# A two-layer gated cross-attention and expert kernel: when GpSimd runs beside VectorE, how the slot one-hots are made, and what the first loads and the first tile share the queues with

## The reference

```python
x = x + tanh(g_xattn[0]) * L0_xattn(layernorm(x), ctx)      # both sides quantised to fp8 by blocks, then x @ ctx^T
x = x + tanh(g_ffn[0])   * L0_ffn(layernorm(x), ...)        # 8 experts (256x128x256), top 2 by softmax, and a shared one
x = x + tanh(g_xattn[1]) * L1_xattn(layernorm(x), ctx, ctx) # 16 heads, causal
x = x + tanh(g_ffn[1])   * L1_ffn(layernorm(x), ...)        # the long last step:

logits = gelu(x @ rw1) @ rw2                 # router
wgt, idx = top_k(softmax(logits), 2)
for e in range(8):                           # experts 256 x 1024 x 256
    Ye = gelu(x @ w1[e] + b1[e]) @ w2[e] + b2[e]
    Ce = gelu(b1[e]) @ w2[e] + b2[e]         # the output of a token that is not sent to e
    for k in range(2):
        mask = idx[..., k] == e
        out = out + any(mask) * wgt[..., k:k + 1] * where(mask, Ye, Ce)
```

## Time and profile before

| | us |
|---|---|
| median of 3 runs | 431.58 |
| the runs | 429.23 to 432.7 |
| the profiled execution | 430.72 |
| its span (first to last instruction) | 428.8 |
| busy in the span: PE, DVE, ACT, POOL | 319.6, 307.7, 262.0, 166.6 |
| chain that ended last: DVE, PE, issue, ACT, DMA, POOL | 36%, 32%, 11%, 11%, 4%, 3% |
| mean granted TensorE clock | 0.898 of 2.4 GHz |

### The profile page before, as it was taken

One profiled execution on the slowest core, in us unless ns is written; L12 is line 12 of the kernel. 1 busy time (PEld: TensorE's weight loads), 2 busy tenths in 40 slices (PEclk: granted clock), 3 DMA queues, 4 the chain that ended last, 5 costly groups with the idle time before them and its releaser, 6 DMA issues.

```text
span 428.8 us, 8535 instructions
## 1 busy us (share of the span) xinstructions
PE 319.6 (75%) x2638; PEld 216.0 (50%) x2639; DVE 307.7 (72%) x739; ACT 262.0 (61%) x528; POOL 166.6 (39%) x231
## 2 busy tenths in 40 slices
PE   0065988869999968777582511578999999999981
PEld 0054337536477635354341210365777777777760
DVE  3998988863764666759676689466788788888870
ACT  1745656623576476848687598033677777777770
POOL 3041301531284260623671659200355444444422
PEclk9997799989999998979788565678999999999997
DMA  8954000140076073411313535834477777777532
GB/s 265 389 144 136 2 0 2 53 142 2 0 165 233 2 208 72 141 50 51 99 50 99 159 92 147 315 130 171 149 247 248 246 245 245 236 248 233 157 36 24
DMA packets 28097, 60.43 MB, mean 141 GB/s; under 512 B 4401, under 2 KB 19010, under 8 KB 24866
## 3 DMA queue, kind: packets, MB, share of 16 engines
q1 hardware_dynamic: 21186, 52.64, 35.6%
q0 software_dynamic: 4416, 6.13, 8.9%
q10 hardware_dynamic: 2464, 1.27, 1.2%
HBM read 27.43 MB, written 6.32 MB: 79 GB/s over the span
## 4 chain that ended last, share of the span: by engine, by line
DVE 36%; PE 32%; issue 11%; ACT 11%; DMA 4%; POOL 3%; ACTq 1%; DVEq 0%; POOLq 0%
PE bank L1202 6%; PE bank L1544 4%; PE bank L1562 4%; ACT arena L1063 4%; DVE MX L1902 4%; DVE arena L2080 2%; PE bank L1547 2%; PE bank L1163 2%; DVE X L1748 2%; ACT arena L1070 2%; DVE arena L2164 2%; DVE arena L2159 2%; PE bank L1565 2%; DVE stats L1626 2%; ACT arena L945 2%
## 5 line engine op out<-in xcount | busy, mean ns | idle before, releaser
L1063 ACT ACTIVATE arena<-arena,B1D 128x128 f32<-128x128 f32 x184 | 57.6, 392 | 14.3 <-DVE arena L2159 13.7
L1562 PE MATMUL bank<-arena 128*128 x184 | 62.3, 385 | 1.2 <-DVE arena L2164 1.2
L2159 DVE TENSOR_REDUCE arena<-bank 128x256 f32<-128x512 f32 x92 | 57.4, 683 | 4.6 <-PE bank L1547 4.6
L663 POOL TENSOR_TENSOR arena<-STG,arena 128x256 f16<-128x256 f32 x56 | 37.1, 695 | 42.4 <-ACT arena L835 42.4
L663 POOL TENSOR_TENSOR W<-STG,W 128x256 f16<-128x256 f32 x64 | 41.4, 683 | 28.3 <-ACT W L835 28.3
L1565 PE MATMUL bank<-arena 128*128 x184 | 50.7, 276 | 0.0
L734 POOL DMA_INDIRECT out_dram<-arena,SI x23 | 37.3, 1621 | 31.0 <-DMA out_dram<-arena,SI 23.7
L721 POOL DMA_INDIRECT arena<-token_rows,GI x23 | 22.8, 991 | 66.5 <-ACT WS L1057 51.3
L2164 DVE SCALAR_TENSOR_TENSOR arena<-arena 128x512 f16<-128x512 f32 x46 | 29.8, 689 | 24.8 <-ACT arena L1070 24.8
L1544 PE MATMUL bank<-arena 128*128 128x256 f16 x256 | 46.4, 281 | 1.5 <-DVE arena L2127 1.1
L1547 PE MATMUL bank<-arena 128*128 128x128 f16 x256 | 45.4, 225 | 0.0
(11 more groups left out here) (266 smaller groups left out, 708.5 us busy)
## 6 DMA issues: line engine op xcount, KB each, us to landing
STG<-in_l_w_dram SPq DMA_DIRECT2D x32, 512.0 KB, 3.6
arena<-W SPq DMA_DIRECT2D x16, 1024.0 KB, 5.0
STG<-W SPq DMA_DIRECT2D x7, 1024.0 KB
arena<-in_l_w_dram SPq DMA_DIRECT2D x2, 1280.0 KB, 12.2
X<-in_x_dram SPq DMA_DIRECT2D x2, 512.0 KB, 6.1
W<-in_ctx_t_dram ACTq DMA_DIRECT2D x2, 512.0 KB, 11.2
W<-in_ctx_dram SPq DMA_DIRECT2D x1, 1024.0 KB, 17.6
k_parts<-W SPq DMA_DIRECT2D x2, 512.0 KB, 3.3
```

The costliest lines, as they stand in the source:

```text
L663: ins = nc.gpsimd.tensor_tensor(l, src, h, ALU.subtract)
L1063: ins = nc.scalar.activation(x, x, ACT.Gelu, bias=B1D[:, e, c:c + 1], scale=1.0 / (X_SCALE * W_SCALE))
L1562: nc.tensor.matmul(bank[6 + q][:, :], GDL[:, q, 0, c * P:(c + 1) * P], W2[:, e, c].rearrange("p s d -> p (s d)"), start=(c == 0), stop=Fal ...
L2159: v.tensor_reduce(half, o, AX.X, ALU.add).then_inc(s_dadd, 1)
```

## The change

The edits, in order of time:

1. SP issues the first half of `x`, waits until it and the first half of the transposed context (`s_ct[0]`, ACT's first DMA) have landed, and only then issues the second half of `x` and all other loads. ACT waits for the same context half before it issues its other loads.
2. GpSimd's `weights_low(0)` to `weights_low(3)` wait for `choose_gates(1)` (`s_gates` 4).
3. In the router stage GpSimd makes the low half of block 21, then waits for all rows of the layernorm (`s_dhl`). VectorE makes those of blocks 22 to 24 (`VECTOR_BLOCKS`), each in one instruction of 128x1024, behind its last `row_low`. GpSimd goes on with block 25, waits for `EID` before 26 and 27, and makes 28 and 29 between the second and the third gather. ScalarE splits block 24 ahead of the rows 4 to 7.
4. `EID` is made ahead of the slot numbers. `BOH` is multiplied by the token number (one more instruction), and `AOH` is now a plain one-hot made in two instructions of 128x1024, with `SMODF` in fp16.
5. Blocks 30 and 31 are staged in `GD`, a buffer that the first tile uses later, so that their loads wait for the transposed rows and a stored half of the token rows instead of a low half; SP issues them ahead of 28 and 29. SP's second store of token rows now stands before the load of block 26.
6. `transpose_coefficients` and `idle_outputs(1)` move on TensorE from ahead of the first tile to behind its up pass. On VectorE, `rows_t(0)` comes ahead of the coefficients, and the low halves of 30 and 31 stand on either side of it.

```diff
         @block.sync
             def load_weights(i):
-                if i >= 4:
+                if i in LATE_BLOCKS:
+                    sp.wait_ge(s_stg[i % 4], 16 * (i // 4))
+                elif i >= 4:
                     sp.wait_ge(s_wlo, i - 3)
...
+            load_x(0)
+            sp.wait_ge(s_ct[0], 16)
+            sp.wait_ge(s_x[0], 16)
+            load_x(1)
             sp.dma_start(WRAW, w1a.rearrange("p c k h -> p (c k h)")).then_inc(s_w1raw, 16)
...
             store_token_rows(0)
-            for i in range(25, 28):
+            load_weights(25)
+            store_token_rows(1)
+            for i in range(26, 28):
                 load_weights(i)
-            store_token_rows(1)
-            for i in range(28, BLOCKS):
+            sp.wait_ge(s_dt_ps, 2)
+            sp.wait_ge(s_rows, 16)
+            for i in LATE_BLOCKS:
+                load_weights(i)
+            for i in range(28, LATE_BLOCKS[0]):
                 load_weights(i)
@@ gpsimd
-            weights_low(0)
             estimate_rstd(4, 0, 2)
-            for i in range(1, 4):
+            pool.wait_ge(s_gates, 4)
+            for i in range(4):
                 weights_low(i)
...
             weights_low(D_BLOCKS[0])
-            for i in D_BLOCKS[1:4]:
-                weights_low(i)
+            pool.wait_ge(s_dhl, T)
             pool.wait_ge(s_pv, 4 * B)
...
-            for i in D_BLOCKS[4:-2]:
+            pool.wait_ge(s_wlo, VECTOR_BLOCKS[-1] + 1)
+            weights_low(D_BLOCKS[4])
+            pool.wait_ge(s_eid, 1)
+            for i in D_BLOCKS[5:7]:
                 weights_low(i)
...
             for j in range(4):
+                if j == 2:
+                    for i in D_BLOCKS[7:-2]:
+                        weights_low(i)
                 gather_rows(j)
@@ scalar
             act.dma_start(g_raw[:, :], gates2.partition_broadcast(P)).then_inc(s_g, 16)
+            act.wait_ge(s_ct[0], 16)
...
-            for i in D_BLOCKS[:3]:
+            for i in D_BLOCKS[:4]:
                 weights_split(i)
@@ tensor
-            idle_outputs(1)
-            transpose_coefficients()
             pe.wait_ge(s_eid, 1)
             transpose_tile(0, 0, 0, first=True)
...
                 if j == 0:
+                    transpose_coefficients()
+                    idle_outputs(1)
                     idle_outputs(0)
                     fold_groups()
@@ vector
             for t in range(HT, T):
                 row_low(t)
+            for i in VECTOR_BLOCKS:
+                _, hi, lo = weight_block(i)
+                dve.wait_ge(s_whi, i + 1)
+                dve.wait_ge(s_wlo, i)
...
+                v.tensor_tensor(lo, src, hi, ALU.subtract).then_inc(s_wlo, 1)
...
-            v.tensor_tensor(BOH, iota_slot[:, :].unsqueeze(1).broadcast_to([P, 2 * T, TILES]),
-                            flat2(SDIVF).unsqueeze(2).broadcast_to([P, 2 * T, TILES]), ALU.is_equal).then_inc(s_onehot, 1)
-            for i in range(2 * T):
-                ins = v.tensor_scalar(AOH[:, i], iota_p[:, :], SMODF[:, i // 2, i % 2:i % 2 + 1],
-                                      token1[:, i // 2:i // 2 + 1], ALU.is_equal, ALU.mult)
+            step(v.tensor_tensor(BOH, iota_slot[:, :].unsqueeze(1).broadcast_to([P, 2 * T, TILES]),
+                                 flat2(SDIVF).unsqueeze(2).broadcast_to([P, 2 * T, TILES]), ALU.is_equal))
+            v.tensor_tensor(by_token, by_token, token1[:, :].unsqueeze(2).broadcast_to([P, T, 2 * TILES]),
+                            ALU.mult).then_inc(s_onehot, 1)
+            for h in range(2):
+                rows = slice(h * T, (h + 1) * T)
+                v.tensor_tensor(AOH[:, rows], iota_p[:, :].unsqueeze(1).broadcast_to([P, T, P]),
+                                flat2(SMODF)[:, rows].unsqueeze(2).broadcast_to([P, T, P]), ALU.is_equal).then_inc(s_onehot, 1)
```

More of the change, by code:

```diff
@@ L1047, in _ @@
                           DWE[:, :, :].bitcast(U32)).then_inc(s_rows, 16)
-            for i in D_BLOCKS[5:]:
+            for i in D_BLOCKS[6:]:
                 weights_split(i)
@@ L2066, in _ @@
             step(v.tensor_tensor_scan(ENDT[:, 1:E + 1], ones[:, 0:E], NT[:, :], 0.0, ALU.mult, ALU.add))
+            step(v.tensor_tensor(EOF_, iota_slot[:, :].unsqueeze(2).broadcast_to([P, TILES, E]),
+                                 ENDT[:, 1:E + 1].unsqueeze(1).broadcast_to([P, TILES, E]), ALU.is_ge))
+            step(v.tensor_reduce(EIDF[:, :], EOF_, AX.X, ALU.add))
+            v.tensor_scalar(EID[:, :], EIDF[:, :], float(E - 1), None, ALU.min).then_inc(s_eid, 1)
             step(v.tensor_tensor(SLOTQ[:, :, :], bank[4][:, 0:T * E].rearrange("p (t e) -> p t e", e=E),
@@ L2104, in _ @@
                 v.tensor_copy(spread, part[:, :, :].rearrange("p e c -> p c e")).then_inc(s_gb16, 1)
-            dve.wait_ge(s_ne01, 1)
-            step(v.tensor_scalar(ACTV[:, :, :].rearrange("p k e -> p (k e)"), bank[3][:, 0:2 * E], 0.0, None, ALU.is_gt))
+            rows_t(0, 0, first=True)
             chosen = DTOPF[:, :, :].unsqueeze(3).broadcast_to([P, T, 2, E])
@@ L2115, in _ @@
             here()
[L2117 to L2130 removed]
+            late_low(LATE_BLOCKS[1])
             def idle_outputs_out():
```

55 lines of the change are left out of this document (28 added, 27 removed).

## The result

| | before | after |
|---|---|---|
| median, same chip (4 executions each) | 430.81 us | 414.15 us |
| the executions | 429.23 to 432.7 | 413.59 to 415.43 |
| the profiled execution, its span | 430.72, 428.8 | 415.43, 413.7 |
| mean granted TensorE clock of it | 0.898 | 0.904 |

The ratio is 0.9616, 95% interval 0.9567 to 0.9665: 16.7 us off by the medians, 15.1 by the two spans. (A ratio leaves out executions that were clearly slower than the others of the same kernel, so it is not always the quotient of the medians shown.) The profiled execution of the kernel before is one beside the four.

A forecast was written before the change was run, and what follows sets the result against it. No engine is full; hand-overs between engines set the end. 0.5 + 6.4 + 2.1 + 5.0 + 4.1 - 1.4 = 16.7 us off the profiled 430.72 gives 414.0, stated as 414.5 for the median; range 410 to 420.5.

The forecast's parts named there:

- edits without effect: Rival, chance 0.02: slow steps have another cause than GpSimd, middle and router lose nothing, late first loads cost ScalarE: 423.
- Start: First loads: fewer packets beside the first context half bring its landing forward by 0.5 us, ends 0 and 1.0.
- Second half: First experts' second half: without GpSimd's quarters beside rstd and gate choice, gate rows come 6.4 us earlier, bounds 5.2 to 7.3.
- The 1.54 for the rstd steps: First experts' second half: faster rstd steps save 1.74 us, of which 1.54 counts, TensorE's wait for the transposes that follow.
- Router: Router stage: row steps and row lows get faster with GpSimd at rest behind block 21; 2.1 us off, 1.2 to 2.6.
- One-hots: Sorting of tokens, from ENDT to GI: 9.2 us instead of 14.2, so 5.0 off, ends 3.5 and 6.5.
- The 416: One-hots: by the skill page's port lock, VectorE's steps could wait a whole quarter, 0.64 instead of 0.47; sum 1.4 later.
- Gather: First gather: with the weight copies through before it, it takes the median 3.1 us, 4.1 off, bounds 1 and 4.3.
- the gather's own start: Rival, chance 0.12: 7.17 us is what a first gather costs, so it stays slow: 418.6.
- First tile: First tile: small products and coefficients, moved behind the first up pass, lose 1.4 us, up to 3.5.
- GpSimd only moves its shadow: Rival, chance 0.10: quarters hurt where they now run, at gate parts, one-hots and coefficients, and TensorE waits there: 418.4.
- more than counted: Rival, chance 0.06: TensorE idles less and gets 2.4 GHz more, and fp16 one-hots run faster; 3 to 4 us: 411.

The follow-up runs named there:

- u1_loads: The changed kernel with all first loads issued at once again, as before the change: 413.89 us.
- p_fill: The changed kernel plus nine 128x512 products nothing reads, in TensorE's gap ahead of the second half of the idle shares: 409.03 us, ratio to before 0.9537.
- c_full: c_nofill plus the nine additional products of p_fill ahead of the second half of the idle shares: 407.04 us, ratio to before 0.9506.
- u2_quarters: The changed kernel with GpSimd again making the low halves of blocks 0 to 3 beside the second rstd and second choice of gates: 420.05 us.
- p_gather: The changed kernel, but SyncE waits for GI before loading the tile weights, so both copies and the first gather are released together: 413.98 us.
- c_nofill: The changed kernel with sorting and first tile reordered: GpSimd rests from EID to GI, VectorE makes blocks 26 and 27, second tile's weights load later: 411.28 us.
- after_again: The changed kernel itself, unchanged, run again beside three further kernels on one chip: 414.75 us, ratio to before 0.9667.

## Why the prediction was right, term by term

The time came out at 414.15 for 414.5, and the forecast's case is the one that happened. But the sum is right with errors on both sides: on the profiled pair 15.1 us for 16.7. That the medians differ by just the 16.7 that was forecast is luck.

The sum's bounds do not add to the 12 to 20 us that the range was made from: all the low ends together give 7.4 (with 3.5 lost in the first tile), all the high ends 20.3. The 423 of edits without effect is the 8.5 us of the two stages alone; with late loads it would be 426.

**Start, 0.5 forecast, 1.57 measured.** The mechanism was right, the size was wrong and outside its own ends of 0 and 1.0. I took the 27 packets beside 32 in half a microsecond as the whole of the sharing. u1_loads shows that taking the other packets away brings the landing forward by all of the last 1.5 us. ScalarE waited for no late load, as forecast.

**Second half, 6.4 forecast, 6.5 measured, in other parts.** The choice fell to 3.72 to the hundredth, and the down pass to 2.32 (2.4 forecast). The 1.54 for the rstd steps did not come: TensorE's transposes waited for VectorE no longer, but they were behind a down pass that took 6.00 in place of 4.48, at a granted clock of 0.53 to 0.61 from 64 to 68 us. In seven other traces, p_fill and c_full among them, that pass takes 4.48, and the gate rows come at 86.4 to 87.2 in place of 87.96; so the term comes when the clock does not fall there. In its place 0.55 came from the first half, ahead of 66 us, and the gate parts were ready earlier behind the gates. u2_quarters shows the cause, GpSimd, by bringing 7.94 us back. Not every tiny step ends once per quarter, though: beside the quarters of that run the two-input steps, the casts and the steps with a constant take 0.5 to 0.7 us each, while the largest-eight search (0.37 for four) and the index search (0.15) keep the lengths that they have alone.

**Router, 2.1 and 2.46.** Right, and so is the narrow cover: 0.27 us of VectorE's waiting are left.

**One-hots, 5.0 and 5.5.** Each length was right (0.90, 0.89, 1.65 twice). What I had not separated was what the gain is due to: the four cells above give 1 us to the form and most of the rest to GpSimd. The price of 0.47 for VectorE beside a quarter held: 1.65 - 1.18. That GpSimd would keep its 0.64 did not: beside the two `AOH` steps a quarter takes 1.65, about as long as the step (1.69 each; they overlap a little, so 1.65 is half of the pair's 3.30). I had read the 0.64 off steps with one tensor as input; beside the two-input row lows the trace of before already had more, 8.38 us for twelve quarters, 0.84 to 0.85 for each of those beside the row lows:

```profile
234.73 8.38 POOL L663 TENSOR_TENSOR W<-STG,W 128x256 f16<-128x256 f32 x12
```

The Trainium skill, page "SBUF — State Buffer" (section "Who interferes with whom"), says that an instruction of VectorE with two inputs in SBUF contends with GpSimd's reads, and in that both engines pay the trace agrees with it. The 416 that I worked out from that page did not come: the quarters did spread, one to each large step, but VectorE's steps were 0.47 longer and not a whole quarter. GpSimd's slower quarters cost nothing on the path, since they ended at 253.05 and `GI` at 253.18.

**Gather, 4.1 and 3.4.** The likely case, within its bounds. The copies were not 8 us ahead as `EID` is, but 5.0, since SyncE waits for more than `EID`; that was enough. The rival that 7.17 is the gather's own start (418.6) is out by p_gather and the table of six kernels. The gather's issue on GpSimd took 1.87 instead of 1.22, which is most of what is missing.

**First tile, -1.4 and -0.45.** The price was right: 3.68 for the 128 small products instead of 1.93 for 64, and 1.04 for the coefficients. The 1.80 that TensorE stood in front of the fold were not all spared: 1.04 of them are left. What the sum did not see is the up pass ahead of them. It starts 1.11 us behind the transposes instead of 1.67 (why is open: `rows_t(0)` follows the transposes by 0.6 in both), and takes 4.23 us instead of 5.07, since its last part has the full clock. The forecast's worry, VectorE late in front of its first sums, was real, and with it a part of the rival that GpSimd only moves its shadow: beside GpSimd's quarters the coefficients took 3.6 us instead of 1.4, and the first sum starts at 263.63, after TensorE's up pass has ended. c_nofill takes that away: there the first sum starts 1.1 us ahead of the up pass's end.

**What the sum did not have: the clock.** The step that failed is the sentence that the tile loop is untouched and moves as a whole. It moved by 2.8 less. That size belongs to this one execution: in after_again, the same kernel, it moved by 0.8 less (fold at 271.23, the span 413.7 again). Half of the rival "more than counted" was about the clock, with the sign the other way: TensorE idling less would get more clock. In the rows of after it has the half clock in three stretches of dense work (64 to 68, 150 to 156, 276 to 286), each right behind a wait. p_fill and c_full show for the last one that the wait is the cause. The waits are as long before the change, where the clock fell later or not at all behind them; what decides that is open. For the one in the attention, 0.8 of the 1.09, no kernel filled the gap, so there it is argued only (the same 16 transposes and 16 products behind a wait of 1.97 us take longer at 1.2 GHz); the remaining 0.29 is a step of VectorE (L1937) that took 2.03 us beside quarters of GpSimd that both kernels have there. Nor is the 1.09 shown to come of the change: from the gate rows to the last rstd the kernel before takes 138.8 us, the changed kernel 139.9 and 139.8, and the others, all with the same attention, 137.1 to 140.6. The Trainium skill, page "TensorE: Matmul & The Clock Gate" (section "Part 1: The HAM clock gate"), says that the slow clock is the default and that activity releases it; p_fill agrees: 1.00 in place of 0.50, with nothing changed but the additional products and their wait.

## What to carry to other kernels

Where a row of VectorE's small steps is slow, look at GpSimd's row in the same stretch before changing the steps: moving its work to where VectorE waits was worth more here than a better form of the steps, and the best place is where both the moved work and what waits for it have room. A wait of TensorE of 2 us ahead of dense work can cost up to 4.6 us through the half clock, and how much differs between executions of one kernel: try filling such a gap with products that nothing reads, and judge a small gain behind it from more than one trace. Release bulk copies 4 us or more ahead of a small transfer that the path waits for, not with it.

## What was not expected of the hardware

- VectorE and GpSimd beside each other pay in two ways. An fp16 step of 128x128 with one tensor as input takes 0.71 us beside a quarter and 0.30 alone, while GpSimd keeps 0.64 to 0.68. Steps with two inputs, 128x1024, take 1.69 instead of 1.22, and there a quarter takes 1.65.
- Nine products of 128x512 without use, 2.12 us of work in a gap of 2.09, shorten a kernel by 4.2 us (c_full against c_nofill).
- Executions of one unchanged kernel on one core range from 411.2 to 415.5 us, and the fastest has the highest mean clock (0.918; the others 0.890 to 0.907). The down pass at 65 us alone took 4.48 us in p_fill and c_full, 5.44 in u2_quarters, and in the changed kernel itself 6.00 in one execution and 6.58 in another.
